# Differential attention with a mixture of experts on one core: head sums moved from GpSimd to VectorE, and four smaller moves in the order

## The chip, the cores and the metric

The kernel runs on one core of a Trainium2 chip. The metric is the device time of one execution in microseconds: 5963.3 us before the change, the median of three runs (5961.5 to 5970.2).

## What is computed

`x` has 16 images of 256 channels by 1024 pixels. Each goes through three layers. Cut to what matters here:

```python
# layer 1: channel attention through 1x1 convolutions (32 channels), out * gamma + x
# group norm over the channels, then differential attention, 8 heads of 32:
a1 = softmax(einsum('bhqd,bhkd->bhqk', q1, k1) / scale)      # 1024 x 1024 for each head
a2 = softmax(einsum('bhqd,bhkd->bhqk', q2, k2) / scale)
attn = a1 - lam.reshape(1, H, 1, 1) * a2
o = einsum('bhqk,bhkd->bhqd', attn, v)
# o: a norm over groups of 64 channels and all tokens, then y = xn @ out_w.T + out_b, and the residual
# layer 3: a shared expert and 8 routed experts (2 taken for each token), hidden size 128
```

The kernel works on one image after another; a batch in this text is one image.

## The kernel before

All matrices that need more than one pass are split in a high and a low part (`act_hi`, `act_lo`, `w_hi`, `w_lo`). The cost of a batch lies mostly in the attention. It is cut into 16 units (`UNITS`): unit `u` is head `u // 2`, its first softmax where `u` is even, its second where `u` is odd. A unit has 8 key tiles (`NT`) of 128 keys by 1024 queries, each taken in two halves.

For a tile, TensorE computes the scores twice. First with queries on the partitions (L1285), so that VectorE can take each query's maximum (L834); this happens 12 tiles ahead (`AHEAD`) and goes through a ring of two PSUM slots of two banks. The list `RING` has its order: projections, scores and, once per unit, a `turn` (L1291), which transposes the eight columns of maxima; VectorE splits the turned rows in a high and a low part (L843, L844) and a DMA puts them into the operand of the second score. Then with keys on the partitions (L1363), the maximum already subtracted; ScalarE takes the exponential (L579) into one of four `probs` buffers. TensorE multiplies them with the values (`weighted`, L1306) into bank 6 or 7 of PSUM, by the unit's parity.

The softmax's denominators are sums of the eight tiles' exponentials. A unit's tiles form two groups (`sum_groups`): tiles 0 to 3 and 4 to 7. GpSimd adds a group's tiles onto each other (L423, 128x1024), five such adds per unit; the sixth, tile 4 + tile 5, is VectorE's (`pair_sum`, L930). Unit 15 is different: VectorE does its sums (`last_sum`, L964). TensorE turns a group's sum into a column sum on all rows (`add_up`, L1313), for the first group at the end of the unit and for the second at pair 1 of the unit behind. A pair is two tiles; `beside_score(u, kt)` and `ahead_of_score(u, kt)` list what VectorE does beside the maximum issued at tile `kt` of unit `u`.

When both denominators are there, VectorE takes the reciprocals in two parts (`sum_recips`, L855) and, at tile 7 of the unit behind (`HEAD_AT`), multiplies (`head_out`): for an even unit into `o_head` (L865), for an odd one, with minus lambda, into a scratch tile `ot` (L870). GpSimd then adds the two (`add_head`, L399), in its queue at the start of unit `2h + 3`, and VectorE takes the head's statistics (`head_statistics`, L876) at the start of an even unit. Head 7's sum is VectorE's own (L1001). `o_free` counts both products and tells TensorE that the bank may be written again; `oh_ready` counts finished heads, for the DMAs that lay the head out by channels.

The norm over heads 0 to 3 needs sums over four heads' statistics (`norm_sums(0)`, L883 to L888, on 8 elements), which VectorE does in unit 15 behind pair 0 (`NORM_AT`). TensorE waits for them behind unit 15's fourth score (`norm_groups`, L1255), and then comes `add_up(14, 1)`.

A batch begins with three projections in the ring (`proj` 0 to 2), each of two halves; ScalarE takes the high part of both halves when the whole item is there (L516, L518, `project`), VectorE the low part (L829), and DMAs on SP's queue lay both out into the stacks (L295 to L306). In unit 0, `weighted(0, 0)` and the score of tile 2 stand ahead of the ring's item for the maximum of (1, 6).

The last tiles of all (`k > TAIL`) alternate between two pairs of banks, and each score there waits for the exponentials of two tiles before.

Of the kernel before, what the change touches and what calls it, by code (L numbers as in the profile page):

```python
# [16 lines left out]
NT = N // P  # L17
# [22 lines left out]
def alone(u):  # L40
# [7 lines left out]
LAST_ADDED = [kt for group in sum_groups(UNITS - 1) for kt in group[1:]]  # L48
# [22 lines left out]
def adds(tile):  # L71

    u, kt = divmod(tile, NT)
    if u == UNITS - 1:
# [5 lines left out]
def last_adds(kt):  # L80

    upto = max([kt] + [group[1] for group in sum_groups(UNITS - 1) if kt == group[0]])
    return sum(at <= upto for at in LAST_ADDED)

# [9 lines left out]
FIRST_VALUES_AT = ((0,), (1, 2), (3, 4), (5, 6))  # L94
# [50 lines left out]
NORM_AT = (UNITS - 1, 0)  # L145
# [3 lines left out]
def build(nc, x, w_split, w_full, out):  # L149
    ctx = ExitStack()  # L150
    with ctx:
# [31 lines left out]
        ot = route[:, 0:4, :].rearrange("p a n -> p (a n)")  # L183
# [60 lines left out]
        sum_pool, sum_pair, sum_last = sem("sum_by_pool"), sem("pair_sum_by_dve"), sem("last_sum_by_dve")  # L244
        ones_done = sem("ones_done")
        o_free, oh_ready = sem("o_free"), sem("o_head_ready")
# [137 lines left out]
        def _(pool):  # L384
# [4 lines left out]
            with pool.Fori(0, B) as b:  # L389
# [34 lines left out]
                add_head(HEADS - 2)  # L424

        @block.scalar
        def _(act):
# [77 lines left out]
            with act.Fori(0, B) as b:  # L505
# [47 lines left out]
                for u in range(UNITS):  # L553
                    for kt in range(NT):
# [9 lines left out]
                        if k >= NP:  # L564
# [100 lines left out]
        def _(dve):  # L665
# [136 lines left out]
            with dve.Fori(0, B) as b:  # L802
# [54 lines left out]
                def head_out(u):  # L857
# [3 lines left out]
                    if u % 2 == 0:  # L861
# [3 lines left out]
                        v.tensor_tensor(oh[:, h % 2, :], ps[:, bank, 0:CQ], rec[:, :], ALU.mult).then_inc(o_free, 1)  # L865
                    else:
                        if h:

                            dve.wait_ge(oh_ready, b * HEADS + h)
                        v.scalar_tensor_tensor(ot[:, :], ps[:, bank, 0:CQ], nlam[:, h:h + 1], rec[:, :],  # L870
                                               ALU.mult, ALU.mult).then_inc(o_free, 1)
# [68 lines left out]
                def beside_score(u, kt):  # L940

                    if u and kt == 3:
                        sum_recips(u - 1, 0)
                    if u < UNITS - 1 and kt == 5:
                        pair_sum(u)
                    if u == UNITS - 1 and kt == NT - 2:
                        last_sum(1, 5)
# [5 lines left out]
                def last_sum(g, kt):  # L953

                    u, group = UNITS - 1, sum_groups(UNITS - 1)[g]
# [3 lines left out]
                    if kt == group[1]:  # L959
                        dve.wait_ge(ones_done, b * ONES + n - NS + 1)  # L960
                    else:
                        dve.wait_ge(sum_last, b * len(LAST_ADDED) + last_adds(kt) - 1)
                    first = probs[:, (k - 1) % NP, :] if kt == group[1] else total
                    v.tensor_tensor(total, first, probs[:, k % NP, :], ALU.add).then_inc(sum_last, 1)  # L964
# [11 lines left out]
                for u in range(UNITS):  # L976
                    for pair in range(PAIRS):
# [11 lines left out]
                        if (u, pair) == NORM_AT:  # L989
                            norm_sums(0)  # L990
                        if u == UNITS - 1:
                            for g, at in (((0, 1),), ((0, 2),), ((1, 4),), ())[pair]:
                                last_sum(g, at)
# [6 lines left out]
                dve.wait_ge(o_free, (b + 1) * UNITS)  # L1000
                v.tensor_tensor(oh[:, (HEADS - 1) % 2, :], oh[:, (HEADS - 1) % 2, :], ot[:, :],  # L1001
                                ALU.add).then_inc(oh_ready, 1)
# [130 lines left out]
        def _(pe):  # L1133
# [103 lines left out]
            first_projection(0, 0)  # L1237
# [20 lines left out]
            def attention(b):  # L1258

                def ring_step(item):  # L1260
# [4 lines left out]
                    if item[0] == "proj":  # L1265
# [6 lines left out]
                        for half in range(NH) if item[1] else ():  # L1272
                            last = split_mm(slot[:, half, :], W_QK + t * CT * C, (C, P),
                                            slice(half * HALF, (half + 1) * HALF))
                    elif item[0] == "part":
# [18 lines left out]
                def weighted(u, kt):  # L1294
# [3 lines left out]
                    if kt == 0 and u >= 2:  # L1298
                        pe.wait_ge(o_free, b * UNITS + u - 1)
# [17 lines left out]
                def add_up(u, g):  # L1317

                    if u == UNITS - 1:
                        pe.wait_ge(sum_last, b * len(LAST_ADDED) + last_adds(sum_groups(u)[g][-1]))  # L1320
                    else:
                        pe.wait_ge(sum_pool, b * len(ADDED) + adds(u * NT + sum_groups(u)[g][-1]))
# [242 lines left out]
```

## Time and profile before

| | |
|---|---|
| three runs | 5970.19, 5963.30, 5961.51 us |
| the profiled execution | 5965.52 us, its span 5963.7 us |
| TensorE busy | 5762.7 us, 97% of the span |
| VectorE busy | 5002.4 us, 84% |
| ScalarE busy | 3258.7 us, 55% |
| GpSimd busy | 2957.8 us, 50% |
| mean granted clock of TensorE | 0.994 |
| time between two batches' first L1363 | 366.4 to 368.8 us |

TensorE's share is near full, but its matmuls are pipelined and their ends are modelled, so a busy TensorE may still have been held up. What tells more is where its instructions stood idle, and the times from one start to the next. GpSimd's 50% is a mean over the batch: it works in the attention alone. The clock is told as a share: 1.00 is 2.4 GHz, and stretches at 0.50 are 1.2 GHz.

### The profile page before, as it was taken

What the parts mean: (1) busy time and instruction counts of PE and PEld (TensorE: products, weight loads), DVE (VectorE), ACT (ScalarE), POOL (GpSimd) and SP (SyncE); (2) the same over time, 40 slices, a digit from 0 to 9 for tenths busy, and PEclk for the clock granted to TensorE, in tenths of its full rate; (3) what the DMA queues carried; (4) which work ended last, traced back from release to release, by engine and by line L of the source; (5) the groups of instructions that cost most, each with busy time, mean ns of one, the idle gap of its engine ahead of it and who ended that gap; (6) DMA issues with size and microseconds to landing.
All of it is one profiled execution on the core that took longest, in us unless ns stands there. A gap on an engine that the chain in (4) does not pass through costs nothing.

```text
span 5963.7 us, 117362 instructions
## 1 busy us (share of the span) xinstructions
PE 5762.7 (97%) x39472; PEld 3674.9 (62%) x39472; DVE 5002.4 (84%) x6839; ACT 3258.7 (55%) x5868; POOL 2957.8 (50%) x1334
## 2 busy tenths in 40 slices
PE   6999999999999999999999999999999999999999
PEld 4566565655657556575665756657566575665656
DVE  5978879798897988979889798897978979788797
ACT  4645546455564655646556465564655646555464
POOL 3816538074380744708347183561825628266281
PEclk9999999999999999999999999999999999999999
DMA  2212222122222222222222221222212222122221
GB/s 78 59 48 62 60 55 54 56 58 58 53 52 62 54 58 55 49 61 58 57 55 50 63 58 55 55 51 63 60 49 56 50 63 59 49 60 50 65 59 47
DMA packets 148810, 338.00 MB, mean 57 GB/s; under 512 B 38624, under 2 KB 61280, under 8 KB 139744
## 3 DMA queue, kind: packets, MB, share of 16 engines
q1 hardware_dynamic: 146400, 329.26, 22.7%
q8 instruction: 313, 5.13, 0.4%
q14 instruction: 305, 2.50, 0.1%
q10 hardware_dynamic: 1792, 1.12, 0.1%
HBM read 90.49 MB, written 17.30 MB: 18 GB/s over the span
## 4 chain that ended last, share of the span: by engine, by line
PE 79%; DVE 10%; issue 6%; DMA 2%; ACT 2%; SPq 0%; DVEq 0%; ACTq 0%
PE psum L1141 18%; PE psum L1363 16%; PE psum L1285 15%; PE psum L1306 14%; PE psum L1460 7%; DVE minus_max L834 5%; PE psum L1313 4%; PE psum L1193 1%; PE psum L1332 1%; PE psum L1414 1%; PE psum L1291 1%; DMA prob_sums<-combine_rows_dram 1%; DMA stack<-stage 1%; DVE small L749 1%; DVE small L886 1%
## 5 line engine op out<-in xcount | busy, mean ns | idle before, releaser
L579 ACT ACTIVATE probs<-psum 128x512 f32<-128x512 f32 x4096 | 2215.8, 595 | 1249.8 <-PE psum L1363 1220.1
L423 POOL TENSOR_TENSOR prob_sums<-prob_sums,probs 128x1024 f32<-128x1024 f32 x960 | 2288.2, 2383 | 475.6 <-DVE prob_sums L930 396.2
L834 DVE TENSOR_REDUCE minus_max<-psum 128x1 f32<-128x1024 f32 x2048 | 2397.8, 1206 | 145.7 <-PE psum L1285 132.7
L1363 PE MATMUL psum<-stack 98*128 98x512 f32 x4096 | 1439.1, 431 | 3.5 <-DVE max_rows L844 3.5
L1285 PE MATMUL psum<-stack 96*128 96x512 f32 x4096 | 1219.4, 406 | 39.7 <-DVE minus_max L834 28.9
L1306 PE MATMUL psum<-probs,v_tokens 128*32 128x256 f32 x16384 | 1112.3, 387 | 0.0
L393 POOL TENSOR_TENSOR stage<-probs,stage 128x512 fp32r<-128x512 f32 x16 | 20.7, 1295 | 2130.9 <-ACT probs L545 2130.9
L1363 PEld LDWEIGHTS psum<-stack 98*128 98x128 f32 x4096 | 712.1, 189 | 541.4 <-ACT probs L579 331.6
L1285 PEld LDWEIGHTS psum<-stack 96*128 96x128 f32 x4096 | 713.8, 189 | 324.5 <-DVE minus_max L834 143.5
L1306 PEld LDWEIGHTS psum<-probs,v_tokens 128*32 128x32 f32 x16384 | 453.0, 110 | 468.1 <-issue 227.4
L423 POOL TENSOR_TENSOR prob_sums<-probs 128x1024 f32<-128x1024 f32 x240 | 573.9, 2391 | 273.3 <-ACT probs L579 273.3
L1141 PE MATMUL psum<-act_hi,w_hi 128*128 128x512 f32 x1730 | 694.2, 401 | 13.0 <-DVE act_lo L813 10.9
L1141 PE MATMUL psum<-act_lo,w_hi 128*128 128x512 f32 x1730 | 682.6, 395 | 0.0
L1141 PE MATMUL psum<-act_hi,w_lo 128*128 128x512 f32 x1730 | 682.2, 394 | 0.0
L634 ACT ACTIVATE probs<-psum 128x512 f32<-128x512 f32 x288 | 172.1, 598 | 685.3 <-PE psum L1141 685.2
L855 DVE RECIPROCAL recip_sum<-psum 128x128 f32<-128x128 f32 x512 | 482.5, 942 | 23.8 <-PE psum L1313 23.2
L1102 DVE SCALAR_TENSOR_TENSOR probs<-probs,psum 128x512 f32<-128x512 f32 x288 | 198.0, 688 | 306.6 <-ACT probs L634 303.8
L1460 PE MATMUL psum<-stack,w_hi 128*128 128x512 f32 x1152 | 419.3, 407 | 8.9 <-DVE stack L1065 8.9
L1141 PEld LDWEIGHTS psum<-act_hi,w_hi 128*128 128x128 f32 x1730 | 324.9, 188 | 118.9 <-DVE act_lo L813 14.7
L1141 PEld LDWEIGHTS psum<-act_lo,w_hi 128*128 128x128 f32 x1730 | 325.4, 188 | 73.5
L1141 PEld LDWEIGHTS psum<-act_hi,w_lo 128*128 128x128 f32 x1730 | 325.6, 188 | 71.7
L930 DVE TENSOR_TENSOR prob_sums<-probs 128x1024 f32<-128x1024 f32 x240 | 355.5, 1481 | 14.0 <-ACT probs L579 14.0
(162 smaller groups left out, 5163.7 us busy)
## 6 DMA issues: line engine op xcount, KB each, us to landing
stack<-stage SPq DMA_DIRECT2D x1024, 128.0 KB, 3.0
stack<-stage SPq DMA_DIRECT2D x256, 256.0 KB, 3.1
prob_sums<-combine_rows_dram SPq DMA_DIRECT2D x128, 256.0 KB, 3.8
stage<-combine_rows_dram SPq DMA_DIRECT2D x128, 256.0 KB, 3.3
x_tile<-x_dram SPq DMA_DIRECT2D x34, 512.0 KB, 3.6
x_tile<-o_head SPq DMA_DIRECT2D x480, 32.0 KB, 1.9
y_dram<-residual SPq DMA_DIRECT2D x16, 512.0 KB, 2.8
y_dram<-stage SPq DMA_DIRECT2D x16, 512.0 KB, 2.9
```

The lines of the kernel that those rows point to most:

```text
L423: nc.gpsimd.tensor_tensor(total, first, probs[:, k % NP, :], ALU.add).then_inc(sum_pool, 1)
L579: nc.scalar.activation(probs[:, k % NP, half * HALF:(half + 1) * HALF], ps[:, exp_bank(k) + half, :], ACT.Exp).then_inc(p_ready, 1)
L834: v.tensor_reduce(nm[:, u % 2, q:q + 1], flat_in, AX.X, ALU.max, negate=True).then_inc(ring_free, 1)
L855: v.reciprocal(rec[:, cols], ps[:, 6 + u % 2, CQ + cols.start:CQ + cols.stop]).then_inc(step, 1)
L930: v.tensor_tensor(psums[:, n % NS, :], probs[:, (k - 1) % NP, :], probs[:, k % NP, :], ALU.add).then_inc(sum_pair, 1)
L1102: link(v.scalar_tensor_tensor(gu, th[:, i % 2, :], 1.0, ps[:, bank, :], ALU.add, ALU.mult))
L1141: ins = mm(dst, wt[:, w + kt * wn[0]:w + kt * wn[0] + wn[1]], xx[:, kt, act_cols], start=(first and n == 0), stop=(last and n == 3 * CT - 1))
L1285: last = mm(slot[:, half, :], stack[0:AUX, s, 0, q * P:(q + 1) * P], stack[0:AUX, s, 1, half * HALF:(half + 1) * HALF], start=True, stop=True)
L1306: last = mm(ps[HD * c:HD * c + HD, bank, 0:CQ], vt[:, kt, HD * h:HD * h + HD], probs[:, k % NP, c * CQ:(c + 1) * CQ], start=(kt == 0), sto ...
L1313: ins = mm(ps[HD * c:HD * c + HD, 6 + u % 2, CQ:2 * CQ], ones[:, :], tile[:, c * CQ:(c + 1) * CQ], start=False, stop=last, skip_group_chec ...
L1363: mm(ps[:, exp_bank(k) + half, :], stack[0:KS, s, 1, kt * P:(kt + 1) * P], stack[0:KS, s, 0, half * HALF:(half + 1) * HALF], start=True, s ...
L1460: last = mm(ps[:, t, :], wt[:, col:col + P], hx[:, i % 2, :], start=(e == 0 and n == 0), stop=(e == NE - 1 and n == 2))
```

## The change

VectorE adds a head itself. The second product of a head is written back into the PSUM bank it comes from, and a second instruction adds `o_head` to it, into `o_head`. GpSimd's `add_head` and the scratch tile go. The count `o_free` is split in three: `o_first` for the first product, `o_second` between the two new instructions, `oh_ready` for the finished head; TensorE and `sum_recips` wait on the first or the last of these by parity. `head_statistics` moves from the start of even units to behind the second maximum of odd ones.

In unit 14, tiles 6 and 7 are added by VectorE (`BY_DVE`), behind its pair sum, with the head's product and sum between them. `norm_sums(0)` moves to unit 14, between the pair sum and tile 6's add. `norm_groups(0)` stays where it was in TensorE's order.

Each projection's first half has a count of its own (`proj_half`), so that ScalarE can take it before the second half is computed; VectorE no longer waits for the whole item, since it waits for ScalarE's halves in any case.

In unit 0, TensorE issues the first score of pair 1's ring items ahead of tile 2's score, and the first weighted sum behind it.

```diff
+BY_DVE = ((UNITS - 2) * NT + 6, (UNITS - 2) * NT + 7)
 ADDED = [u * NT + kt for u in range(UNITS - 1) for group in sum_groups(u) for kt in group[1:]
-         if kt != sum_groups(u)[1][1]]
+         if kt != sum_groups(u)[1][1] and u * NT + kt not in BY_DVE]
...
-FIRST_VALUES_AT = ((0,), (1, 2), (3, 4), (5, 6))
+FIRST_VALUES_AT = ((), (1, 2), (3, 4), (5, 6))
...
-NORM_AT = (UNITS - 1, 0)
+NORM_AT = (UNITS - 1, 1)
...
-                def add_head(h):
-
-                    pool.wait_ge(o_free, b * UNITS + 2 * h + 2)
-                    nc.gpsimd.tensor_tensor(oh[:, h % 2, :], oh[:, h % 2, :], ot[:, :],
-                                            ALU.add).then_inc(oh_ready, 1)
-
                 for u in range(UNITS - 1):
-                    if u % 2 and u >= 3:
-                        add_head((u - 3) // 2)
...
-                    act.wait_ge(ring_full, b * len(RING) + RING_AT["proj", t] + 1)
                     for half in range(NH):
+                        if half:
+                            act.wait_ge(ring_full, b * len(RING) + RING_AT["proj", t] + 1)
+                        else:
+                            act.wait_ge(proj_half, b * 3 + t + 1)
...
-                            if k - NP >= (UNITS - 1) * NT:
+                            if k - NP >= BY_DVE[0]:
 
-                                act.wait_ge(sum_last, b * len(LAST_ADDED) + last_adds(kt - NP))
+                                act.wait_ge(sum_dve, b * len(LAST_ADDED) + last_adds(k - NP))
...
-                    dve.wait_ge(ring_full, b * len(RING) + n + 1)
+                    if item[0] != "proj":
+                        dve.wait_ge(ring_full, b * len(RING) + n + 1)
...
-                            dve.wait_ge(o_free, b * UNITS + u)
+                            dve.wait_ge(oh_ready if u % 2 == 0 else o_first, b * HEADS + (u + 1) // 2)
...
-                        v.scalar_tensor_tensor(ot[:, :], ps[:, bank, 0:CQ], nlam[:, h:h + 1], rec[:, :],
-                                               ALU.mult, ALU.mult).then_inc(o_free, 1)
+                        v.scalar_tensor_tensor(ps[:, bank, 0:CQ], ps[:, bank, 0:CQ], nlam[:, h:h + 1], rec[:, :],
+                                               ALU.mult, ALU.mult).then_inc(o_second, 1)
+                        dve.wait_ge(o_second, b * HEADS + h + 1)
+                        v.tensor_tensor(oh[:, h % 2, :], ps[:, bank, 0:CQ], oh[:, h % 2, :],
+                                        ALU.add).then_inc(oh_ready, 1)
...
-                    if u % 2 == 0 and u >= 4 and kt == 0:
-                        head_statistics((u - 4) // 2)
...
+                    if u % 2 and u >= 3 and kt == 1:
+                        head_statistics((u - 3) // 2)
...
+                    if u == UNITS - 2 and kt == 5:
+                        norm_sums(0)
+                    if u == UNITS - 2 and kt == 6:
+                        last_sum(u, 1, 6)
...
                     if u and kt == HEAD_AT:
                         head_out(u - 1)
-                    if u == UNITS - 1 and kt == NT - 1:
-                        head_statistics(HEADS - 2)
+                    if u == UNITS - 2 and kt == 7:
+                        last_sum(u, 1, 7)
...
-                        pe.wait_ge(o_free, b * UNITS + u - 1)
+                        pe.wait_ge(oh_ready if u % 2 else o_first, b * HEADS + u // 2)
...
+                            if k == 2:
+                                ring_step(BESIDE[u, pair][0])
                             for half in range(NH):
...
+                            if k == 2:
+                                weighted(0, 0)
```

## Rows read from the trace of the kernel before

**Rows 1.** TensorE's waits over the run: us in total, times, longest.

```profile
PE psum L1255 <- DVE small L888: 33.3, 16, 2.1
PE psum L1285 <- DVE minus_max L834: 28.9, 96, 0.4
PE psum L1291 <- DVE minus_max L834: 21.0, 32, 0.7
PE psum L1414 <- DVE act_hi L1014: 16.1, 16, 1.0
```

**Rows 2.** Timeline, units 14 and 15, batch 5: start, length, instruction, idle before.

```profile
2151.70 2.57 DVE L930 TENSOR_TENSOR prob_sums<-probs 128x1024 f32<-128x1024 f32 x1 [0.88 <-ACT probs L579]
...
2154.51 4.81 POOL L423 TENSOR_TENSOR prob_sums<-prob_sums,probs 128x1024 f32<-128x1024 f32 x2 [1.32 <-ACT probs L579]
2154.59 2.33 DVE L883 COPY small<-small 128x8 f32<-128x8 f32 x1
...
2156.05 1.46 PE L1363 MATMUL psum<-stack 98*128 98x512 f32 x4
...
2157.02 2.31 DVE L886 SCALAR_TENSOR_TENSOR small<-small 128x8 f32<-128x8 f32 x1
...
2159.37 0.17 DVE L888 TENSOR_REDUCE small<-small 128x4 f32<-128x16 f32 x1
...
2159.59 0.38 PE L1255 MATMUL psum<-small,w_full 128*128 128x4 f32 x2 [2.08 <-DVE small L888]
2159.91 0.64 PE L1313 MATMUL psum<-prob_sums,ones 128*32 128x256 f32 x8
```

**Rows 3.** Windows: length, each engine's busy time, granted clock (PEclk), DMA share, GB/s.

```profile
core 0: us, PE busy (x) PEld busy (x) DVE busy (x) ACT busy (x) POOL busy (x), PEclk, DMA share, GB/s
2158.00:2164.00 6.00, 4.41 (x37) 2.44 (x38) 5.83 (x6) 1.33 (x4) 1.99 (x2) 0.72 0.09 23
1423.00:1429.00 6.00, 4.16 (x54) 2.22 (x54) 5.95 (x6) 2.85 (x6) 2.25 (x2) 1.00 0.09 23
2176.00:2182.00 6.00, 4.99 (x25) 3.55 (x23) 4.60 (x11) 3.41 (x6) 0.00 (x0) 1.00 0.45 115
```

**Rows 4.** Timeline of VectorE, units 8 to 10, batch 5.

```profile
2066.80 0.22 DVE L843 CAST max_rows<-psum 8x128 fp32r<-8x128 f32 x1
...
2077.12 2.36 DVE L834 TENSOR_REDUCE minus_max<-psum 128x1 f32<-128x1024 f32 x2 [0.47 <-PE psum L1285]
...
2080.26 0.24 DVE L843 CAST max_rows<-psum 8x128 fp32r<-8x128 f32 x1
...
2083.81 1.88 DVE L930 TENSOR_TENSOR prob_sums<-probs 128x1024 f32<-128x1024 f32 x1
...
2094.34 0.28 DVE L843 CAST max_rows<-psum 8x128 fp32r<-8x128 f32 x1
```

**Rows 5.** Timeline of GpSimd in unit 9 of batch 5.

```profile
2076.58 0.74 POOL L399 TENSOR_TENSOR o_head<-o_head,route 128x256 f32<-128x256 f32 x1
...
2079.75 4.86 POOL L423 TENSOR_TENSOR prob_sums<-prob_sums,probs 128x1024 f32<-128x1024 f32 x2
```

**Rows 6.** Timeline of TensorE at the starts of units 9 and 10, batch 5.

```profile
2076.46 1.09 PE L1285 MATMUL psum<-stack 96*128 96x512 f32 x4
...
2088.01 0.73 PE L1285 MATMUL psum<-stack 96*128 96x512 f32 x2 [0.26 <-DVE minus_max L834]
```

**Rows 7.** Groups of VectorE by form over the run: count, busy us, mean ns, idle before.

```profile
L870 DVE SCALAR_TENSOR_TENSOR route<-psum,minus_lambda,recip_sum 128x256 f32<-128x256 f32 x128 | 60.0, 469 | 0.6
L865 DVE TENSOR_TENSOR o_head<-psum,recip_sum 128x256 f32<-128x256 f32 x128 | 52.2, 408 | 0.0
L964 DVE TENSOR_TENSOR prob_sums<-prob_sums,probs 128x1024 f32<-128x1024 f32 x32 | 38.1, 1190 | 1.7
L1001 DVE TENSOR_TENSOR o_head<-o_head,route 128x256 f32<-128x256 f32 x16 | 6.8, 425 | 0.6
```

**Rows 8.** Timeline of VectorE at the start of batch 6's attention.

```profile
2293.45 2.36 DVE L834 TENSOR_REDUCE minus_max<-psum 128x1 f32<-128x1024 f32 x2 [0.31 <-PE psum L1285]
...
2311.73 2.36 DVE L834 TENSOR_REDUCE minus_max<-psum 128x1 f32<-128x1024 f32 x2 [0.94 <-PE psum L1285]
```

More of the change, by code:

```diff
@@ L45 @@
 ONES = UNITS * GROUPS + 1
+BY_DVE = ((UNITS - 2) * NT + 6, (UNITS - 2) * NT + 7)
 ADDED = [u * NT + kt for u in range(UNITS - 1) for group in sum_groups(u) for kt in group[1:]
-         if kt != sum_groups(u)[1][1]]
-LAST_ADDED = [kt for group in sum_groups(UNITS - 1) for kt in group[1:]]
+         if kt != sum_groups(u)[1][1] and u * NT + kt not in BY_DVE]
+LAST_ADDED = list(BY_DVE) + [(UNITS - 1) * NT + kt for group in sum_groups(UNITS - 1) for kt in group[1:]]
 LN_EPS = 1e-5
@@ L73, in adds @@
     u, kt = divmod(tile, NT)
-    if u == UNITS - 1:
+    if u == UNITS - 1 or tile in BY_DVE:
         return len(ADDED)
@@ L77, in adds, with last_adds @@
     return sum(at <= u * NT + upto for at in ADDED)
-def last_adds(kt):
-    upto = max([kt] + [group[1] for group in sum_groups(UNITS - 1) if kt == group[0]])
-    return sum(at <= upto for at in LAST_ADDED)
+def last_adds(tile):
+    u, kt = divmod(tile, NT)
+    upto = max([kt] + [group[1] for group in sum_groups(u) if kt == group[0]])
+    return sum(at <= u * NT + upto for at in LAST_ADDED)
 def ones_after(u, pair):
@@ L945, in beside_score, with last_sum @@
                         pair_sum(u)
+                    if u == UNITS - 2 and kt == 5:
+                        norm_sums(0)
+                    if u == UNITS - 2 and kt == 6:
+                        last_sum(u, 1, 6)
                     if u == UNITS - 1 and kt == NT - 2:
[L947 removed]
+                        last_sum(u, 1, 5)
                     if u and kt == HEAD_AT:
                         head_out(u - 1)
[L950 to L955 removed]
+                    if u == UNITS - 2 and kt == 7:
+                        last_sum(u, 1, 7)
+                def last_sum(u, g, kt):
+                    group = sum_groups(u)[g]
                     n, k = u * GROUPS + g, u * NT + kt
@@ L958, in last_sum @@
                     dve.wait_ge(p_ready, b * 2 * UNITS * NT + 2 * k + 2)
-                    if kt == group[1]:
+                    if u < UNITS - 1 and kt == group[2]:
+                        dve.wait_ge(sum_pair, b * (UNITS - 1) + UNITS - 1)
+                    elif kt == group[1]:
                         dve.wait_ge(ones_done, b * ONES + n - NS + 1)
                     else:
-                        dve.wait_ge(sum_last, b * len(LAST_ADDED) + last_adds(kt) - 1)
+                        dve.wait_ge(sum_dve, b * len(LAST_ADDED) + last_adds(k) - 1)
                     first = probs[:, (k - 1) % NP, :] if kt == group[1] else total
-                    v.tensor_tensor(total, first, probs[:, k % NP, :], ALU.add).then_inc(sum_last, 1)
+                    v.tensor_tensor(total, first, probs[:, k % NP, :], ALU.add).then_inc(sum_dve, 1)
                 def k2_low_part():
@@ L988, in _ @@
                             beside_score(u, at)
-                        if (u, pair) == NORM_AT:
-                            norm_sums(0)
                         if u == UNITS - 1:
                             for g, at in (((0, 1),), ((0, 2),), ((1, 4),), ())[pair]:
-                                last_sum(g, at)
+                                last_sum(u, g, at)
                 norm_variance(0)
@@ L1274, in ring_step @@
                                             slice(half * HALF, (half + 1) * HALF))
+                            if half == 0:
+                                last.then_inc(proj_half, 1)
                     elif item[0] == "part":
@@ L1317, in add_up @@
                 def add_up(u, g):
-                    if u == UNITS - 1:
-                        pe.wait_ge(sum_last, b * len(LAST_ADDED) + last_adds(sum_groups(u)[g][-1]))
+                    last = u * NT + sum_groups(u)[g][-1]
+                    if last in LAST_ADDED:
+                        pe.wait_ge(sum_dve, b * len(LAST_ADDED) + last_adds(last))
                     else:
-                        pe.wait_ge(sum_pool, b * len(ADDED) + adds(u * NT + sum_groups(u)[g][-1]))
+                        pe.wait_ge(sum_pool, b * len(ADDED) + adds(last))
                     ones_mm(u, psums[:, (u * GROUPS + g) % NS, :], g == len(sum_groups(u)) - 1).then_inc(ones_done, 1)
@@ L1365, in attention @@
                                    stop=True).then_inc(st_full, 1)
-                            for item in BESIDE[u, pair][slice(0, 2) if kt % 2 == 0 else slice(2, None)]:
+                            if k == 2:
+                                weighted(0, 0)
+                            for item in BESIDE[u, pair][slice(int(k == 2), 2) if kt % 2 == 0 else slice(2, None)]:
                                 if item[0] != "turn":
                                     ring_step(item)
-                        if (u, pair) == (NORM_AT[0], NORM_AT[1] + 1):
+                        if (u, pair) == NORM_AT:
                             norm_groups(b, 0)
```

18 lines of the change are left out of this document (6 added, 12 removed).

## The prediction

> **What bounds the kernel now.** First the waits of TensorE over the run [rows 1]: it waits little, so only a shorter wait, a shorter instruction stream or a higher clock can move the end. Four entries matter here: 33.3 us on the norm sums (L888) in 16 waits, one per batch, up to 2.1 us; 28.9 us on row maxima in 96 waits, six per batch; 21.0 us for the turn (L1291) in 32; and 16.1 us on `act_hi`, which the change doesn't touch.
>
> The first is read in the timeline around the end of unit 14 of batch 5 (batches and units counted from 0) [rows 2]. TensorE is through with unit 15's fourth score at 2157.5 (2156.05 + 1.46) and stands until 2159.59. The norm's `L883` and `L886`, on 8 elements, take 2.33 and 2.31 us: each starts just behind the start of a GpSimd add of `L423` and ends just behind that add's end, while `L888`, with none beside it, takes 0.17. GpSimd's two adds run from 2154.51 to 2159.32, so `add_up(14, 1)` (L1313, 2159.91) was not to be had sooner either: two chains end together, and removing one alone would bring nothing.
>
> Then the clock. Behind that wait the granted clock of a 6 us window is 0.72; in batch 3, behind an equal wait, it is 1.00 [rows 3]. Of 16 such windows, one per batch, 12 lie at 0.72 to 0.78 and 4 at 1.00. A stretch at the 1.2 GHz level instead of 2.4 costs (1 - 0.72) x 6 = 1.68 us.
>
> Then a unit in the middle. VectorE's turns (L843) at 2066.80, 2080.26 and 2094.34 put one unit at 13.46 us and the next at 14.08 [rows 4]. In the long one's run-up `L930`, the pair sum, took 1.88 us, from 2083.81. GpSimd's second and third adds run from 2079.75 for 4.86 us, to 2084.61, and the pair sum ends 1.08 behind that; they in turn stood behind an add of a head (L399, 0.74 us at 2076.58) [rows 5]. GpSimd rests only for some 1.3 us around each pair sum: its five adds (2.43 each, start to start) and that rest make 13.45 us, as long as TensorE's unit, and each `L399` is beyond it. So the maximum comes late and TensorE waits 0.26 at 2088.01 and is some 0.6 us behind in all [rows 6]. This is so at the start of units 4, 10, 12 and 14 of each batch.
>
> **The change part by part.** The sum is made against the profiled execution, 5965.5 us (span 5963.7 and 1.8 around it), 2.2 above the median of the three runs.
>
> *Unit 14's second group and the norm sums.* Counted on the clock of rows 2: the pair sum ends at 2154.27 as now (the third add of GpSimd holds it, and both move with TensorE). Behind it GpSimd is idle, so the norm's four instructions take 4 x 0.17 = 0.65, to 2154.9. Then `last_sum` of tile 6, by the price of `L964` 1.2 us, to 2156.1; the head's product and sum 0.47 + 0.04 + 0.41, to 2157.0; `last_sum` of tile 7, to 2158.25 [rows 2, 7]. `add_up(14, 1)` starts at 2158.3 and not at 2159.91: 1.6 us per batch, 25.6 us. What is late next is this chain on VectorE, 0.8 us behind TensorE's 2157.5. Queued behind it are head 6's statistics, unit 15's first sum and the reciprocals; the last wait for `add_up(14, 1)` anyway. ScalarE's exponentials of tiles (15, 2) and (15, 3) wait for these two sums at 2156.1 and 2158.25, where GpSimd delivered at 2156.9 and 2159.3. Bounds: 1.0 (a sum that meets a late GpSimd add) to 2.1 (nothing left to wait for). I take 1.6, the chain's own sum.
>
> *The clock.* A wait of 0.8 is left where 2.1 was. The nearest rows are the 16 waits of up to 1.0 us at `L1414` [rows 1]; the window behind one of them shows 1.00 [rows 3]. So it should stay at 2.4 GHz: 12 x 1.68 = 20.2 us. Bounds 0 and 20.2; I take the whole, since 0.8 is nearer to 1.0 than to 2.1.
>
> *Heads added by VectorE.* GpSimd loses 7 adds of 0.74 per batch; its third adds then end about 0.7 earlier in odd units, the pair sums cost 1.2 again, and the four late unit starts (0.6 each) go: 2.4 us. Against it each odd product now issues a wait and an add: 0.04 + 0.41 (by `L865`, one operand from PSUM) [rows 7]. Behind them in VectorE's queue stand the first two maxima of an odd unit, and TensorE waits for these. In unit 9 the second ended at 2077.12 - 0.47 = 2076.65, and TensorE took its buffer at 2076.46 + half of 1.09 = about 2076.95 [rows 4, 6]: 0.3 to spare for 0.45, so 0.15 late, and 0.05 for starting again. That is 0.2 at units 9, 11 and 13, and about 0.3 at 3 and 5, where GpSimd runs closer behind TensorE: 1.1 us in all. Unit 7 has projection matmuls beside it, unit 15 is in the term above. Head statistics behind the second maximum fall in the 0.47 that VectorE idles there: nothing; with that cover gone, 0.33 each. No row has a VectorE instruction that writes PSUM. I take the 469 ns of the same instruction into SBUF (`L870`), nearest in form; bounds 0.41 (`L865`) and 1.19 (`L964`, four times the elements), the upper one left to rival (d). The weighted sums that wait for the new counts stand behind the unit's fourth score in TensorE's order, by then they are long there: nothing. At the end of the batch `L1001` gives way to the same add from PSUM: nothing. Net 2.4 - 1.1 = 1.3, 20.8 us; bounds -0.6 and 2.3 per batch.
>
> For the add alone, the Trainium skill speaks against reading PSUM ("VectorE: DVE Perf Modes", the TRN2 errata): 120 + 256 cycles at 0.96 GHz, an estimate of 392 ns, against 58 + 256, 327 ns, from SBUF. The trace disagrees: 408 ns with PSUM, 425 without [rows 7]. By the page the adds would be 65 ns dearer than from SBUF, 7 us over the run if none were hidden; the sum goes by the rows.
>
> *Halves counted singly.* ScalarE's first half starts before the second is there, and a projection is through 0.6 sooner. VectorE's first step of a batch can't use it, the later ones and the stack's DMAs can: they are issued 0.6 sooner on SP's queue, in the old order. VectorE idles 0.31 before its first maximum of the batch [rows 8], and from there runs maxima without a break; that 0.31 is the gain, 0.3 (bounds 0 and 0.5).
>
> *Unit 0's maximum moved.* VectorE idles 0.94 at 2311.73 since the score comes behind the weighted sum and a score that waits for an exponential [rows 8]. Issued ahead of both, its maximum follows at once, and the second wait for the turn (about 0.6 of L1291's 1.3 per batch) goes. But GpSimd's first add of the batch starts no sooner, and its third holds the pair sum where it is, so units 1 to 3 get some back: 0.45, bounds 0 and 0.75. Together 0.75, 12.0 us.
>
> Sum: 25.6 + 20.2 + 20.8 + 12.0 = 78.6; 5965.5 - 78.6 = 5886.9, and 2.2 less for the median: about 5885.
>
> **The rivals.** (a) The stall moves instead of going: odd units start 0.6 late, five per batch, where four even ones did. For it: VectorE idles only 0.47 at such a start [rows 4]. Against: 1.2 us come back by the pair sum and the statistics. The heads then cost 0.6 per batch and don't bring 1.3: 1.9 x 16 = 30 us more, 5915. (b) The clock still drops, as the chain on VectorE is longer than I think or the drop doesn't need the whole 2.1 us: 20 us more, 5905. (c) The two parts at the start do nothing, since GpSimd or the loop's own start holds them (its first step may come later than any count it waits for): 12 us more, 5897. The change then does not do what its last words say. (d) Slower: the product that writes PSUM and the add that reads it back cost X more than 0.92 us. Nothing is left to hide X at seven heads of 16 batches, 112 X in all; it eats the 78 us from X = 0.7, and shows as slower than before at 0.8. At 1.0 the time is 5997. Against it: the add form that reads PSUM is within 20 ns of the one that doesn't [rows 7].
>
> **How the numbers follow.** Forecast 0.70, (a) 0.13, (b) 0.08, (c) 0.04, (d) 0.02, and 0.03 for a wait not seen. The predicted time is the forecast's, 5885. With its terms between their bounds, though not all at one end at once, it spans about 5862 to 5908; the range reaches over (a), (b) and (c) to 5922 and leaves out some 0.15. A measurement of this kernel can tell about 0.2%, 12 us, from no change. Faster 0.95 (the forecast, a, b, c and part of the rest), same 0.02, slower 0.03.
>
> **What would show it.** Right: `L1255`'s wait of 2.1 gone, and one of about 0.5 at the matmuls of `add_up` behind it; clock 1.00 in all 16 windows; the norm's copy at 0.17; pair sums at about 1.2 to 1.3 in every middle unit; no late start at units 4, 10, 12, 14, and short ones at odd units; the product into PSUM near 0.47 and its add near 0.41; the second turn without its 0.6. Wrong: pair sums of 1.8 that remain, or odd starts late by 0.5; an add of 0.6 or more; a window below 1.00.

## The result, and the profile after

The changed kernel took 5879.1 us (median; 5877.0 to 5879.6), the kernel before beside it 5964.5. The ratio is 0.9855, with a 95% interval of 0.9838 to 0.9872: 85 us less, where 79 less were forecast. The profiled execution's span is 5877.4 us and its mean granted clock 0.997. A batch takes 362.1 us now, from its first tile score (the one with keys on the partitions, L1363 before and L1365 now) to the next batch's, where most took 368.0.

TensorE's waits over the run, changed kernel (us in total, times, longest):

```profile
PE psum L1418 <- DVE act_hi L1011: 16.4, 16, 1.0
PE psum L1284 <- DVE minus_max L830: 12.8, 32, 0.4
PE psum L1290 <- DVE minus_max L830: 11.1, 16, 0.7
...
PE psum L1312 <- DVE prob_sums L966: 6.0, 16, 0.4
...
PE psum L1252 <- DVE small L884: 3.2, 16, 0.2
```

Against [rows 1]: the norm sums' 33.3 us are 3.2, and these belong to the second norm at the end of the attention. The waits for maxima fell from 96 to 32, and those left stand at the start of unit 0 or just ahead of it. The turn waits once per batch, not twice. A new wait of 0.38 us stands at the column sum.

The end of unit 14 in batch 5, some lines of VectorE and TensorE (start, length, instruction, idle before), to be laid beside [rows 2]:

```profile
2121.82 2.47 DVE L926 TENSOR_TENSOR prob_sums<-probs 128x1024 f32<-128x1024 f32 x1 [0.85 <-ACT probs L574]
...
2124.22 0.16 DVE L879 COPY small<-small 128x8 f32<-128x8 f32 x1
...
2124.48 0.17 DVE L882 SCALAR_TENSOR_TENSOR small<-small 128x8 f32<-128x8 f32 x1
...
2124.88 1.23 DVE L966 TENSOR_TENSOR prob_sums<-prob_sums,probs 128x1024 f32<-128x1024 f32 x1
...
2126.03 0.49 DVE L863 SCALAR_TENSOR_TENSOR psum<-psum,minus_lambda,recip_sum 128x256 f32<-128x256 f32 x1
...
2126.55 0.43 DVE L866 TENSOR_TENSOR o_head<-psum,o_head 128x256 f32<-128x256 f32 x1
...
2126.89 1.21 DVE L966 TENSOR_TENSOR prob_sums<-prob_sums,probs 128x1024 f32<-128x1024 f32 x1
...
2127.50 0.28 PE L1252 MATMUL psum<-small,w_full 128*128 128x4 f32 x2
...
2128.15 0.64 PE L1312 MATMUL psum<-prob_sums,ones 128*32 128x256 f32 x8 [0.38 <-DVE prob_sums L966]
```

The norm's copy takes 0.16 us where it took 2.33. From the pair sum's end (2124.29) to the column sum (2128.15) the chain is 3.86 us long; it was 5.64 (2154.27 to 2159.91). Two windows of the changed kernel, in batches 5 and 0, for [rows 3]; the last three numbers are granted clock, DMA share and GB/s:

```profile
2126.00:2132.00 6.00, 5.62 (x66) 2.90 (x58) 5.96 (x9) 4.61 (x10) 0.00 (x0) 1.00 0.09 23
319.00:325.00 6.00, 6.00 (x76) 2.88 (x68) 5.83 (x10) 4.66 (x9) 0.00 (x0) 1.00 0.05 14
```

The clock stays at 2.4 GHz here, in unit 15, in all 16 batches. VectorE in units 8 to 10 of batch 5, for [rows 4]:

```profile
2038.34 0.21 DVE L839 CAST max_rows<-psum 8x128 fp32r<-8x128 f32 x1
...
2045.25 0.47 DVE L863 SCALAR_TENSOR_TENSOR psum<-psum,minus_lambda,recip_sum 128x256 f32<-128x256 f32 x1
2045.76 0.42 DVE L866 TENSOR_TENSOR o_head<-psum,o_head 128x256 f32<-128x256 f32 x1
2046.10 2.35 DVE L830 TENSOR_REDUCE minus_max<-psum 128x1 f32<-128x1024 f32 x2
2048.36 0.42 DVE L872 BATCH_NORM_STATS2 small<-o_head 128x6 f32<-128x256 f32 x1
...
2051.91 0.28 DVE L839 CAST max_rows<-psum 8x128 fp32r<-8x128 f32 x1
...
2055.49 1.20 DVE L926 TENSOR_TENSOR prob_sums<-probs 128x1024 f32<-128x1024 f32 x1
...
2065.44 0.24 DVE L839 CAST max_rows<-psum 8x128 fp32r<-8x128 f32 x1
```

From turn to turn it is 13.57 and 13.53 us, where [rows 4] has 13.46 and 14.08; the pair sum of unit 9 takes 1.20 us and not 1.88. The head's two instructions by form, for [rows 7] (count, busy us, mean ns, idle before):

```profile
L863 DVE SCALAR_TENSOR_TENSOR psum<-psum,minus_lambda,recip_sum 128x256 f32<-128x256 f32 x128 | 61.1, 477 | 0.6
L866 DVE TENSOR_TENSOR o_head<-psum,o_head 128x256 f32<-128x256 f32 x128 | 54.4, 425 | 4.4
```

The product written into PSUM takes 477 ns, against 469 into SBUF.

The start times of the tile scores give each stretch of a batch (us, medians over the batches). Units that are not listed moved by less than 0.03.

| stretch | before | after | per batch |
|---|---|---|---|
| unit 0 | 14.09 | 13.73 | -0.36 |
| units 4, 10, 12, 14 | 14.09, 14.08, 14.11, 12.64 | 13.48, 13.47, 13.48, 12.12 | -2.37 |
| units 3, 5, 9, 11, 13 | 13.50, 17.84, 13.49, 13.48, 13.49 | 13.65, 18.01, 13.64, 13.56, 13.65 | +0.71 |
| unit 15, clock at 1.00 | 10.45 | 8.56 | -1.89 |
| unit 15, mean of 16 batches | 11.62 | 8.56 | -1.17 beyond the row above |
| last score to the next batch's first | 140.51 | 140.00 | -0.51 |

### The profile page after: what moved, and what is told of

It is laid out like the page before. It is cut to its first block, busy times and chain, and to the rows that moved or that the text cites. A ratio compares the mean times of both kernels' runs of the same rounds, so it can differ in the third digit from the quotient of the medians.

```text
span 5877.4 us, 116994 instructions
## 1 busy us (share of the span) xinstructions
PE 5734.4 (98%) x39472; PEld 3668.8 (62%) x39472; DVE 4968.9 (85%) x6983; ACT 3260.7 (55%) x5868; POOL 2802.4 (48%) x1190
## 4 chain that ended last, share of the span: by engine, by line
PE 88%; DVE 6%; issue 3%; DMA 2%; ACT 1%; SPq 0%; DVEq 0%; ACTq 0%
PE psum L1138 19%; PE psum L1365 18%; PE psum L1284 17%; PE psum L1305 16%; PE psum L1464 7%; PE psum L1312 5%; DVE minus_max L830 1%; PE psum L1190 1%; PE psum L1332 1%; PE psum L1418 1%; PE psum L1290 1%; DMA prob_sums<-combine_rows_dram 1%; DVE small L744 1%; DVE prob_sums L966 1%; PE psum L1203 1%
## 5 line engine op out<-in xcount | busy, mean ns | idle before, releaser
L417 POOL TENSOR_TENSOR prob_sums<-prob_sums,probs 128x1024 f32<-128x1024 f32 x928 | 2210.6, 2382 | 475.8 <-DVE prob_sums L926 418.6
L1365 PE MATMUL psum<-stack 98*128 98x512 f32 x4096 | 1432.0, 430 | 4.7 <-DVE max_rows L840 4.7
L1305 PE MATMUL psum<-probs,v_tokens 128*32 128x256 f32 x16384 | 1100.1, 384 | 0.0
L1365 PEld LDWEIGHTS psum<-stack 98*128 98x128 f32 x4096 | 708.0, 188 | 544.3 <-ACT probs L574 343.0
L851 DVE RECIPROCAL recip_sum<-psum 128x128 f32<-128x128 f32 x512 | 482.6, 943 | 20.8 <-PE psum L1312 20.3
L1464 PE MATMUL psum<-stack,w_hi 128*128 128x512 f32 x1152 | 419.3, 407 | 9.8 <-DVE stack L1062 9.8
L926 DVE TENSOR_TENSOR prob_sums<-probs 128x1024 f32<-128x1024 f32 x240 | 318.0, 1325 | 13.5 <-ACT probs L574 13.5
```

Of the source, the lines that this page charges most:

```text
L417: nc.gpsimd.tensor_tensor(total, first, probs[:, k % NP, :], ALU.add).then_inc(sum_pool, 1)
L851: v.reciprocal(rec[:, cols], ps[:, 6 + u % 2, CQ + cols.start:CQ + cols.stop]).then_inc(step, 1)
L926: v.tensor_tensor(psums[:, n % NS, :], probs[:, (k - 1) % NP, :], probs[:, k % NP, :], ALU.add).then_inc(sum_pair, 1)
L1305: last = mm(ps[HD * c:HD * c + HD, bank, 0:CQ], vt[:, kt, HD * h:HD * h + HD], probs[:, k % NP, c * CQ:(c + 1) * CQ], start=(kt == 0), sto ...
L1365: mm(ps[:, exp_bank(k) + half, :], stack[0:KS, s, 1, kt * P:(kt + 1) * P], stack[0:KS, s, 0, half * HALF:(half + 1) * HALF], start=True, s ...
L1464: last = mm(ps[:, t, :], wt[:, col:col + P], hx[:, i % 2, :], start=(e == 0 and n == 0), stop=(e == NE - 1 and n == 2))
```

## The experiments

All of them start from one of the two kernels and undo or do one part. Times of runs with an interval are medians beside the kernel before on the same chip; runs of one execution are compared by their span with the changed kernel's 5877.4. The first batch's first tile score comes at 99.1 to 102.1 us in the 13 traces (100.5 in the changed kernel), so such a comparison is good to a microsecond or two. A "fall" is a stretch of TensorE's clock at 1.2 GHz within unit 15.

**Heads back on GpSimd.** Undone in the changed kernel: where the heads are added, and with that the statistics' place.

```diff
+                def add_head(h):
+                    pool.wait_ge(o_second, b * HEADS + h + 1)
+                    nc.gpsimd.tensor_tensor(oh[:, h % 2, :], oh[:, h % 2, :], ot[:, :],
+                                            ALU.add).then_inc(oh_ready, 1)
...
-                        dve.wait_ge(o_second, b * HEADS + h + 1)
-                        v.tensor_tensor(oh[:, h % 2, :], ps[:, bank, 0:CQ], oh[:, h % 2, :],
-                                        ALU.add).then_inc(oh_ready, 1)
```

> The changed kernel with only the heads' sums undone: GpSimd adds them again (its scratch tile, its place in the queue and the statistics at even starts as before); unit 14's sums, the norm sums, the halves and the moved maximum stay changed. Theory (GpSimd's adds are the chain that made units 4, 10, 12 and 14 late): those four starts are late by 0.6 us again, pair sums in units 3, 9, 11 and 13 take 1.8 to 1.9 us, the short lateness of odd units (0.1 to 0.17 in the changed kernel) is gone; 1.57 us per batch, 25 us over the run, so about 5904 us and a ratio of 0.990 to the kernel before. Rival (the adds cost VectorE what they save GpSimd): within 5 us of the changed kernel, ratio 0.9855.

It took 5898.4 us, ratio 0.9885 (0.9869 to 0.9902): 19 us of the gain gone, not 25. TensorE's waits, and VectorE's pair sums in units 8 and 9 of batch 5:

```profile
PE psum L1300 <- DVE minus_max L841: 29.1, 96, 0.4
```

```profile
2049.83 1.21 DVE L937 TENSOR_TENSOR prob_sums<-probs 128x1024 f32<-128x1024 f32 x1
...
2063.32 1.88 DVE L937 TENSOR_TENSOR prob_sums<-probs 128x1024 f32<-128x1024 f32 x1
```

The 96 waits are back, units 4, 10, 12 and 14 take 14.10, 14.10, 14.11 and 12.63 us, units 3, 9, 11 and 13 take 13.48 to 13.51, unit 5 17.87. The theory holds in the units (1.71 us per batch). What it missed is unit 15: 8.21 us where the changed kernel has 8.56, with no wait at the column sum. The head's add, moved to VectorE, stands in the chain behind unit 14 and costs 0.35 there.

**Only the heads, on the kernel before.** The same part done alone.

```diff
-                        v.scalar_tensor_tensor(ot[:, :], ps[:, bank, 0:CQ], nlam[:, h:h + 1], rec[:, :],
-                                               ALU.mult, ALU.mult).then_inc(o_free, 1)
+                        v.scalar_tensor_tensor(ps[:, bank, 0:CQ], ps[:, bank, 0:CQ], nlam[:, h:h + 1], rec[:, :],
+                                               ALU.mult, ALU.mult).then_inc(o_second, 1)
+                        dve.wait_ge(o_second, b * HEADS + h + 1)
+                        v.tensor_tensor(oh[:, h % 2, :], ps[:, bank, 0:CQ], oh[:, h % 2, :],
+                                        ALU.add).then_inc(oh_ready, 1)
```

> The kernel before with only the heads' sums moved to VectorE (in place in PSUM, statistics behind the second maximum of odd units); all else as before. Theory (heads are worth 1.57 us per batch on their own): 25 us faster than the kernel before, about 5939, ratio 0.9958; TensorE's wait at the norm's matmul and the low clock stay. Rival (GpSimd's chain is only freed together with the rest): within 8 us of the kernel before.

5939.8 us, ratio 0.9954 (0.9938 to 0.9971), 27 us less than before: the heads bring their gain alone. The units give 24 us of it (1.51 per batch), by the start times of the tile scores. TensorE's waits:

```profile
PE psum L1244 <- DVE small L880: 34.5, 32, 2.0
PE psum L1282 <- DVE minus_max L826: 21.0, 32, 0.7
...
PE psum L1276 <- DVE minus_max L826: 12.7, 32, 0.4
```

The wait at the norm's matmul is still 2.0 us, but the clock fell in 7 of 16 batches, not in 12. Unit 15 took 10.34 us without a fall and 12.0 with one, and 13.0 in three batches where the low stretch was twice as long; in the mean the clock cost 0.91 us per batch, where it cost 1.17 before. That is 4 of the 27 us, and the heads' work is not the whole of the 27.

**The load on GpSimd alone.** An add of the old size, of constants into an unused tile, at the six places where heads stood; VectorE as in the changed kernel.

```diff
+                    nc.gpsimd.tensor_tensor(spare[:, :], wf[:, 0:CQ], wf[:, CQ:2 * CQ],
+                                            ALU.add).then_inc(spare_done, 1)
```

> The changed kernel with an add of the old size (128x256, constants into an unused tile) back in GpSimd's queue at the six old places; VectorE's work is untouched. Theory (GpSimd's chain alone makes the even starts late): pair sums of 1.8 us return in units 3, 9, 11 and 13 and units 4, 10, 12 and 14 start 0.4 to 0.6 us late, on top of the short lateness of odd units: 2.0 to 2.4 us per batch, 32 to 38 us. Rival (what mattered was VectorE's wait for GpSimd's head or the place of the statistics): no change.

One execution, span 5908.7: 31 us more. In unit 9 of batch 5, GpSimd's and VectorE's rows from the timeline:

```profile
2059.68 0.74 POOL L406 TENSOR_TENSOR route<-w_full 128x256 f32<-128x256 f32 x1
...
2062.83 4.85 POOL L430 TENSOR_TENSOR prob_sums<-prob_sums,probs 128x1024 f32<-128x1024 f32 x2
...
2067.07 1.69 DVE L939 TENSOR_TENSOR prob_sums<-probs 128x1024 f32<-128x1024 f32 x1
```

GpSimd's third add ends at 2067.68 and the pair sum 1.08 behind it, as in the kernel before. Units 4, 10, 12 and 14 are 0.37 to 0.45 longer than in the changed kernel, 26 of the 31 us; the rest is 0.12 in unit 15, a little in odd units, and a first batch that starts 1.2 us later. Units 9 and 10 together take 27.52 us, as with the add in the kernel before (27.57) and with the heads given back (27.59), and 27.11 without it. This settles the cause: 0.74 us more on GpSimd is enough, with nothing changed on VectorE.

**A dearer head on VectorE.** One more instruction of the same form in front of each head's add.

```diff
                         dve.wait_ge(o_second, b * HEADS + h + 1)
+                        v.tensor_tensor(spare[:, :], ps[:, bank, 0:CQ], oh[:, h % 2, :], ALU.add)
```

> The changed kernel with one more VectorE instruction of 128x256 in front of each head's add (the same sum into an unused tile): the head costs about 0.38 us more, as if reading or writing PSUM were dearer. Theory (nothing is left to hide it at odd starts): units 3, 5, 9, 11 and 13 start later by 0.4 us more each and the sum chain of unit 14 by 0.35, together 2.3 us per batch, 37 us over the run. Rival (VectorE still has slack within the pair of units): under 10 us.

Span 5913.2: 36 us more. TensorE's waits:

```profile
PE psum L1286 <- DVE minus_max L831: 27.0, 96, 0.4
...
PE psum L1314 <- DVE prob_sums L968: 11.1, 16, 0.7
```

Units 3, 5, 9, 11 and 13 took 0.31 to 0.34 more, unit 15 took 0.33 more. The stretch between the batches, where head 7 is added, took 0.29 more. The added instruction takes 0.34 us of VectorE's time from its start to the next one's, so it is paid in full: rival (d)'s price, 112 X, is confirmed (with X about 0.33, 37 us), but the change itself had no such X.

**Unit 14's second group back on GpSimd**, the norm sums left in unit 14.

```diff
-BY_DVE = ((UNITS - 2) * NT + 6, (UNITS - 2) * NT + 7)
+BY_DVE = ()
```

> The changed kernel with unit 14's tiles 6 and 7 added by GpSimd again; the norm sums stay in unit 14 behind the pair sum. Theory (two chains ended together, and one alone brings nothing): TensorE waits for GpSimd's second add instead, some 1.9 us, the clock falls again in about 12 of 16 batches, and about 50 us come back: 5925 to 5930 us, ratio 0.994. Rival (the norm sums were the only chain that counted): under 10 us slower than the changed kernel, ratio 0.987 or less.

5921.2 us, ratio 0.9923 (0.9907 to 0.9940): 42 us slower than the changed kernel, where the theory said 50 and the rival under 10. TensorE's waits:

```profile
PE psum L1308 <- POOL prob_sums L417: 25.9, 16, 1.7
```

The wait has another name now: the same matmul group waits 1.6 us for GpSimd. The clock fell in 14 of 16 batches.

**The norm sums back in unit 15**, the second group left with VectorE.

```diff
-                    if u == UNITS - 2 and kt == 5:
-                        norm_sums(0)
...
+                        if (u, pair) == (UNITS - 1, 0):
+                            norm_sums(0)
```

> The changed kernel with the norm sums back in unit 15 behind pair 0; tiles 6 and 7 of unit 14 stay with VectorE. Theory (the norm's small instructions took 2.3 us each only because GpSimd was adding beside them; it rests now): they take 0.17 us each there too, TensorE's wait for them is 0.8 to 1.0 us and no window falls below clock 1.00; 0.6 us per batch, 10 us slower than the changed kernel, about 5889, ratio 0.987. Rival (their place is what counts): the wait of 2 us at the norm's matmul returns, 40 us or more slower.

5899.1 us, ratio 0.9889 (0.9872 to 0.9905): 20 us slower, not 10. Timeline of VectorE and TensorE in unit 15 of batch 5, and two windows (batches 2 and 3):

```profile
2135.85 0.17 DVE L879 COPY small<-small 128x8 f32<-128x8 f32 x1
...
2136.13 0.17 DVE L882 SCALAR_TENSOR_TENSOR small<-small 128x8 f32<-128x8 f32 x1
...
2136.55 0.39 PE L1252 MATMUL psum<-small,w_full 128*128 128x4 f32 x2 [0.96 <-DVE small L884]
```

```profile
1045.00:1051.00 6.00, 5.03 (x57) 2.71 (x57) 5.61 (x10) 3.54 (x9) 0.00 (x0) 1.00 0.10 26
1408.00:1414.00 6.00, 5.16 (x42) 2.68 (x46) 4.72 (x9) 2.11 (x5) 0.00 (x0) 0.72 0.07 20
```

The small instructions take 0.17 us in their old place: it was GpSimd beside them, not the place, as the theory said, and the wait is 0.96 as forecast. But the clock fell behind it in 6 of 16 batches, which the expectation denied: 0.59 us per batch, 9 of the 20.

**Both undone.** The two diffs together.

> The changed kernel with both undone: GpSimd adds tiles 6 and 7 of unit 14, and the norm sums stand in unit 15. Theory: as with the first alone, since either chain holds TensorE to the same time: 1.9 us of waiting per batch and 1.65 us of low clock in about 12 batches, 50 us slower than the changed kernel, about 5929, within 5 us of the run that undoes the group alone. Rival (the two add up): this one is the sum of the two single ones.

5934.4 us, ratio 0.9947 (0.9931 to 0.9964): 55 us slower than the changed kernel. This is neither theory: 13 more than the group alone, and less than 42 + 20. The waits are 1.62 and 1.97 us, and the clock fell in 16 batches instead of 14, in two of them for twice as long: 0.35 x 16 for the wait, 2 x 1.6 for two more falls and 2 x 1.25 for the long ones make 11 of the 13. As GpSimd and the norm's instructions stand in the kernel before, the two chains end within 0.35 us of each other, the norm's later.

Read from this run, each of the two parts alone does bring something: with the other parts of the change in place, the norm sums moved alone bring 13 us (5934.4 to 5921.2) and the group alone 35 (5934.4 to 5899.1). The prediction's "removing one alone would bring nothing" is not so. The two chains are tied: once GpSimd rests, the norm's instructions take 0.17 us each instead of up to 2.3, so moving the group shortens both.

**The halves counted together again.**

```diff
-                        if half:
-                            act.wait_ge(ring_full, b * len(RING) + RING_AT["proj", t] + 1)
-                        else:
-                            act.wait_ge(proj_half, b * 3 + t + 1)
```

> The changed kernel with ScalarE and VectorE waiting for the whole projection again. Theory: from a batch's last score to the next one's first 0.45 us more (140.4 and not 140.0), as VectorE's first maximum starts 0.3 to 0.5 us later; 7 us over the run. Rival (it is hidden behind the loop's own start): 140.0 as in the changed kernel.

Span 5894.7: 17 us more, not 7. From last score to first it is 140.65 us, 0.65 more; TensorE's wait for the stack's DMAs is back:

```profile
PE psum L1280 <- DMA stack<-stage: 9.3, 16, 1.0
```

Another 0.3 us per batch lies where nothing was changed: unit 11 takes 13.69 and not 13.56, unit 15 8.75 and not 8.56. At both places the instruction behind a head's add on VectorE starts later, by 0.11 and 0.18 us, though nothing that it is seen to wait for is later. The same 13.69 is in the run that does the heads alone, which has these VectorE waits too. So some 5 of the 17 us are not the halves' work; that they hang on which waits stand further up in VectorE's program is a guess from these two runs, and why is open. Another 3 us are not the halves' either: its first batch starts 1.4 us later, and in batch 12 the clock was at 1.2 GHz for a stretch behind a wait of 2.3 us in the experts (for VectorE's `stack`, L1062 in the changed kernel), some 1.5. The halves themselves are worth the 0.65 per batch, 10 us.

**Unit 0's order as before.**

```diff
-                            if k == 2:
-                                ring_step(BESIDE[u, pair][0])
...
-                            if k == 2:
-                                weighted(0, 0)
```

> The changed kernel with unit 0's order as before (first weighted sum and tile 2's score ahead of the ring's item). Theory: VectorE's idle 0.9 us and TensorE's second wait for a turn, 0.6 us, return; unit 0 takes 14.08 us and not 13.72, and GpSimd's hold on unit 0's pair sum keeps it from being more: 6 us over the run. Rival (GpSimd holds the unit whatever the order): 13.72 as in the changed kernel.

Span 5885.5: 8 us more, 6 of them in unit 0 and some 2 in batch 12, where the clock fell as in the run before. Unit 0 takes 14.09, and the second turn's wait is back (TensorE's waits):

```profile
PE psum L1290 <- DVE minus_max L830: 21.0, 32, 0.7
```

**A longer wait.** One reciprocal of 128x128 into an unused tile ahead of unit 14's last sum.

```diff
                     if u == UNITS - 2 and kt == 7:
+                        v.reciprocal(spare[:, 0:128], rec[:, 0:CQ // 2])
                         last_sum(u, 1, 7)
```

> The changed kernel with one reciprocal of 128x128 into an unused tile ahead of unit 14's last sum on VectorE. Theory: TensorE's wait at the column sum grows by 0.87 us, to about 1.25, and the clock falls in some batches, more than the 6 of 16 seen at 0.97 us and fewer than the 14 seen at 1.6; 14 us for the wait and 1.2 to 1.7 us for each such batch, 25 to 35 us in all. Rival (a wait under 1.6 us seldom lowers the clock): 14 us.

Span 5903.9: 27 us more, as the theory said. The wait is 1.17 us and the clock fell in 8 of 16 batches; unit 15 took 9.36 us without a fall and 10.95 with one:

```profile
PE psum L1314 <- DVE prob_sums L968: 18.8, 16, 1.2
```

**The head's add later.** The first experiments say that the add costs TensorE at odd starts and in unit 14's chain, and that VectorE idles behind the second maximum.

```diff
                     if u % 2 and u >= 3 and kt == 1:
-                        head_statistics((u - 3) // 2)
+                        add_head((u - 3) // 2)
+                    if u % 2 == 0 and u >= 4 and kt == 1:
+                        head_statistics((u - 4) // 2)
+                    if u == UNITS - 1 and kt == NT - 1:
+                        head_statistics(HEADS - 2)
```

> The changed kernel with the head's add taken off its product: the product into PSUM stays at tile 7 of the even unit, the add comes behind the second maximum of the odd unit, where VectorE idles 0.47 us, and the statistics behind the second maximum of the next even unit. Theory (odd units are late only since the add stands ahead of their first two maxima): units 3, 5, 9, 11 and 13 lose their 0.1 to 0.17 us, and the chain behind unit 14's pair sum ends 0.4 earlier, so that TensorE's wait of 0.38 at the column sum goes; 0.8 + 0.38 = 1.2 us per batch, 19 us, about 5861. Rival (VectorE's gap is filled and the third maximum comes late instead): within 5 us of the changed kernel.

5860.6 us, ratio to the kernel before 0.9824 (0.9811 to 0.9838): faster than both kernels, 18 us faster than the changed one, as the theory said. VectorE at the start of unit 9 of batch 5:

```profile
2038.30 0.47 DVE L863 SCALAR_TENSOR_TENSOR psum<-psum,minus_lambda,recip_sum 128x256 f32<-128x256 f32 x1
2038.85 2.36 DVE L830 TENSOR_REDUCE minus_max<-psum 128x1 f32<-128x1024 f32 x2
2041.12 0.41 DVE L869 TENSOR_TENSOR o_head<-psum,o_head 128x256 f32<-128x256 f32 x1
2041.69 2.36 DVE L830 TENSOR_REDUCE minus_max<-psum 128x1 f32<-128x1024 f32 x2 [0.16 <-PE psum L1292]
```

The add lies in what was idle time, of which 0.16 us is left. Units 3, 5, 9, 11 and 13 take 13.48, 17.84, 13.50, 13.43 and 13.46 us, unit 15 8.12, and no wait is left at the column sum.

## Why the prediction was right

**Unit 14 and the norm.** Forecast 1.6 us per batch, measured 1.89. Both chains held TensorE: each undone alone makes it wait again. But they are not independent, as the run with both undone shows, and there the text was wrong. The chain from the pair sum's end was worked out as 4.0 us (2154.27 to 2158.3) and is 3.86, so that `add_up` comes 1.78 us sooner; the wait left over is 0.38, not 0.5 to 0.8. The last 0.1 of the 1.89 is not traced to an instruction.

**The clock.** Forecast 20.2 us. Unit 15's mean was 11.62 and a batch without a fall took 10.45, so the falls cost 1.17 x 16 = 19 us (1.56 each, not 1.68, as not every window stood at 0.72), and all of it went. The amount is right; the step to it was weak. It argued from the waits of 1.0 at `L1414` that a wait of 0.8 does no harm. With the norm sums back in unit 15 a wait of 0.97 was followed by a fall in 6 batches; waits of 0.36 to 0.69, in four runs and the changed kernel, were followed by none. No run has the 0.8 that the forecast was made for. With a wait of 0.38 the question did not arise, and to that extent this term held by luck.

**The heads.** Forecast 2.4 - 1.1 = 1.3, measured 2.37 - 0.71 = 1.66 in the units. The four late starts went whole, and the run with a load on GpSimd alone shows that they were GpSimd's. At odd starts 0.15 was worked out before the 0.05 for starting again: 0.15, 0.15, 0.08 and 0.16 were measured at 3, 9, 11 and 13, and 0.17 at 5. The extra 0.1 put on units 3 and 5 for a GpSimd close behind was wrong; its pair sums took 1.20 and 1.22 there. The price of the new instructions was right (477 and 425 ns for 469 and 408). By the TRN2 errata table in "VectorE: DVE Perf Modes" of the Trainium skill, an instruction that reads PSUM takes 120 cycles of 0.96 GHz and one for each element, an estimate of 392 ns for this add. The trace disagrees: it took 425 ns, the same as the add without PSUM in [rows 7].

**The halves.** Forecast 0.3, measured 0.5 from the stretch between the batches and 0.65 by undoing it. VectorE's first maximum was put forward by the 0.3 that it idled, as worked out; not counted was that TensorE also lost its wait for the stack's DMAs, and that the whole start moves with the first projections. **The maximum.** Forecast 0.45, measured 0.36; the pair sum of unit 0 is held by GpSimd (it takes 1.76 us now, 1.39 before), as the text said.

The sum by measured terms is 30.2 + 18.7 + 26.6 + 8.2 + 5.8 = 89.5 us; the spans differ by 86.3. Of the 3 us between, 0.7 is a later start of the first batch, 0.5 that the stretch between batches comes 15 times and not 16, and 0.4 a longer wait in batch 12 (1.9 us at L1464, where 1.5 was the longest before). The rest is open. Against the forecast of 25.6, 20.2, 20.8 and 12.0, unit 14 and the heads each brought about 5 us more.

**The rivals.** (a), odd units late by 0.6: they are late by 0.15; the run with a dearer head puts them at 0.48. (b), the clock: not here, but real at a wait of 1 us. (c), parts that do nothing: each is worth about 6 us or more. (d), slower: its price per microsecond holds, its X is 0.02.

## What to carry to other kernels

Look for a second engine's chain whose period equals the bound's: it shows little idle time and little waiting anywhere, yet every extra instruction on it delays the engine that shares a step with it. Where two chains end together, take from both, and check by giving each back alone and both at once: only the last told what each is worth alone. Work that must move to a busy engine belongs in that engine's idle time within the cycle, not behind the instruction that makes its operand: the same add cost 18 us in one place and nothing 2.8 us later.

## What the runs showed of the hardware

In the kernel before, VectorE's copy and its `scalar_tensor_tensor` on 8 elements in SBUF took 2.33 and 2.31 us beside a GpSimd add, and each ended with that add. Without one they took 0.16 to 0.17 us, at two places in the program. With the heads alone moved, the copy starts later within GpSimd's add and takes 1.30. A pair sum on VectorE that meets a GpSimd add ends 1.08 us behind it (before, and with the load on GpSimd).

The granted clock fell from 2.4 to 1.2 GHz in some of the batches behind a single wait of TensorE in unit 15, and whether it falls is not a matter of the wait's length alone:

| run | wait, mean us | batches with a fall, of 16 |
|---|---|---|
| unit 0's order as before | 0.36 | 0 |
| changed kernel | 0.38 | 0 |
| load on GpSimd | 0.49 | 0 |
| halves together | 0.55 | 0 |
| a dearer head | 0.69 | 0 |
| norm sums in unit 15 | 0.97 | 6 |
| a longer wait | 1.17 | 8 |
| group on GpSimd | 1.62 | 14 |
| heads alone, on the kernel before | 1.95 | 7 |
| both undone | 1.97 | 16 |
| kernel before | 2.08 | 12 |

Two kernels with waits of 1.95 and 1.97 us differ by 7 and 16, and the waits of 1.0 us at `act_hi`, in each of these kernels, were followed by no low clock. Behind a wait for `stack` in the experts of batch 12 (L1464 in the changed kernel), four runs had one low stretch each, at waits of 1.9 to 2.4 us, and the changed kernel at 1.9 and the heads alone at 2.4 had none. A kernel that loses 2 us to such a wait may lose 1.6 more, at times 2.6, or nothing.
